# Products of q, k and v as three 16-bit products of high and low parts

## The reference

```python
x = x + attention(layernorm(x))
    proj = x @ w_qkv                    # 512 x 1536, split into q, k, v
    q, k = rope(q), rope(k)             # 16 heads of 32
    q, k = layernorm(q), layernorm(k)   # per head, with scale and bias
    a = tril((q @ k.T) ** 4)
    out = (a / a.sum(-1)) @ v
    out = out @ w_out
x = x + experts(layernorm(x))           # 4 of 16 experts a row, and a shared one
```

## Time and profile before

| | us |
|---|---|
| median of 3 runs (lowest, highest) | 1075.78 (1074.30, 1088.98) |
| the profiled execution | 1074.49 |
| its span, from first to last instruction | 1072.7 |
| busy PE, DVE, ACT, POOL in the span | 949.1, 718.1, 571.4, 523.3 |
| product matmuls of L515, busy | 184.2 |

### The profile page before, as it was taken

How to read it: one execution, slowest core, us unless ns; L and a number is a source line. 1 busy time by engine, 2 the same in 40 slices (tenths; PEclk the granted TensorE clock), 3 DMA queues, 4 the chain that set the end, 5 groups by cost and what they waited for, 6 DMA issues and landing times.

```text
span 1072.7 us, 21356 instructions
## 1 busy us (share of the span) xinstructions
PE 949.1 (88%) x5818; PEld 459.0 (43%) x5819; DVE 718.1 (67%) x1635; ACT 571.4 (53%) x1044; POOL 523.3 (49%) x738
## 2 busy tenths in 40 slices
PE   7989999899899989787787899999999999979892
PEld 5443334334443435242354445454544444434440
DVE  3888976887879688749658675565666555545552
ACT  2368984888838984976254234343444443324340
POOL 0007663665526563757201014666676665646642
PEclk9999999999999999857969999999999999999996
DMA  8113334443324433943457988898999897869884
GB/s 305 82 40 118 119 119 143 152 139 136 122 99 158 158 118 128 385 153 124 157 189 247 315 314 214 215 227 209 224 223 228 198 221 200 208 155 219 194 197 68
DMA packets 76795, 193.57 MB, mean 180 GB/s; under 512 B 10048, under 2 KB 11200, under 8 KB 75456
## 3 DMA queue, kind: packets, MB, share of 16 engines
q1 hardware_dynamic: 58816, 149.57, 41.9%
q0 software_dynamic: 17920, 43.26, 20.1%
HBM read 131.71 MB, written 61.10 MB: 180 GB/s over the span
## 4 chain that ended last, share of the span: by engine, by line
PE 37%; DVE 14%; issue 12%; ACT 10%; DMA 10%; POOL 6%; POOLq 4%; DVEq 4%; ACTq 0%; SPq 0%
DMA out<-yy,sidx 9%; PE bank L786 9%; PE bank L515 8%; PE bank L589 5%; PE bank L578 4%; PE bank L807 4%; ACT arena L960 3%; POOL wr L1157 2%; POOLq L1200 2%; PE bank L530 2%; PE bank L777 1%; ACT s_p L952 1%; POOLq L1156 1%; DVE st L1271 1%; POOL s_p L1132 1%
## 5 line engine op out<-in xcount | busy, mean ns | idle before, releaser
L786 PE MATMUL bank<-arena,xgT 128*128 (+1 forms) x1152 | 284.4, 384 | 4.3 <-ACT xgT L1094 3.4
L1132 POOL TENSOR_TENSOR s_p<-s_p,c_causal 128x128 f32<-128x128 f32 x256 | 148.7, 604 | 218.0 <-DVE s_p L1512 186.9
L1087 ACT ACTIVATE hT<-bank 128x512 f16<-128x512 f16 x96 | 57.3, 597 | 289.7 <-PE bank L796 268.6
L515 PE MATMUL bank<-arena 128*128 128x512 f32 x384 | 184.2, 628 | 11.6 <-ACT arena L921 4.6
L1140 POOL TENSOR_TENSOR arena<-arena 128x768 f16<-128x768 f32 x68 | 116.6, 1714 | 95.4 <-ACT arena L864 95.0
L786 PEld LDWEIGHTS bank<-arena,xgT 128*128 128x128 f16 x1152 | 108.2, 98 | 128.0 <-issue 38.1
L1181 POOL DMA_INDIRECT out<-yy,sidx x80 | 128.5, 1606 | 37.6 <-issue 29.2
L807 PE MATMUL bank<-wd,hT 128*128 128x512 f16 x576 | 142.1, 383 | 0.7 <-ACT hT L1087 0.7
L1799 DVE TENSOR_SCALAR yy<-bank,hsc 128x512 f32<-128x512 f32 x80 | 60.0, 751 | 122.9 <-DMA out<-yy,sidx 122.9
L960 ACT ACTIVATE arena<-bank 128x512 f32<-128x512 f32 (+3 forms) x256 | 101.2, 439 | 59.3 <-PE bank L563 59.2
L515 PEld LDWEIGHTS bank<-arena 128*128 128x128 f32 x384 | 73.2, 199 | 102.9 <-issue 88.9
(11 more groups left out here) (187 smaller groups left out, 1398.1 us busy)
## 6 DMA issues: line engine op xcount, KB each, us to landing
wd<-w_scratch SPq DMA_DIRECT2D x82, 512.0 KB
arena<-w_experts SPq DMA_DIRECT2D x34, 768.0 KB, 5.9
w_scratch<-arena SPq DMA_DIRECT2D x34, 768.0 KB, 4.5
arena<-w_scratch SPq DMA_DIRECT2D x17, 1024.0 KB, 7.4
xin<-x SPq DMA_DIRECT2D x4, 1024.0 KB, 5.5
arena<-x SPq DMA_DIRECT2D x4, 1024.0 KB, 5.5
x_scratch<-arena SPq DMA_DIRECT2D x4, 1024.0 KB, 5.1
xg<-xn_scratch SPq DMA_DIRECT2D x16, 256.0 KB, 4.3
```

The lines of the kernel that those rows point to most:

```text
L515: mm = pe.matmul(bk[:], xnT[:, c, m * P:m * P + P], wqkv[:, c, w * E:w * E + E], start=(c == 0), stop=(c == EC - 1))
L786: mm = pe.matmul(bank[2 + k][:], xgT[:, k, xh * EC + c, :], w, start=(c == 0 and xh + wh == 0), stop=(c == EC - 1 and xh == 1))
L1132: pool.tensor_tensor(d, d, C["causal"][:], ALU.mult).then_inc(p4_masked, 1)
```

## The change

Each product becomes three products of 16-bit numbers: high rows with high weights, high rows with low weights, low rows with high weights. The area of `xnT` and `wqkv` holds the high and the low part where it held the fp32 number. The weights and the rows are scaled by powers of two (256 for the weights, `WS`; 1024 for the rows, `XS`), which is taken back where v is copied and by the constants added under the roots.

```diff
             def qkv(b, m, w, bk, done):
-                pe.wait_ge(xT_sb, upto(b, m))
+                pe.wait_ge(xT_lo, upto(b, m))
                 for c in range(EC):
-                    mm = pe.matmul(bk[:], xnT[:, c, m * P:m * P + P], wqkv[:, c, w * E:w * E + E],
-                                   start=(c == 0), stop=(c == EC - 1))
+                    for xh, wh in ((0, 0), (0, 1), (1, 0)):
+                        mm = pe.matmul(bk[:], xnT[:, xh, c, m * P:m * P + P], wqkv[:, wh, c, w * E:w * E + E],
+                                       start=(c == 0 and xh + wh == 0), stop=(c == EC - 1 and xh == 1))
                 mm.then_inc(done, 1)
...
+            def first_lo(b, m, bk):
+                dve.wait_ge(xT_sb, upto(b, m))
+                dve.tensor_tensor(xnT[:, 1, :, m * P:m * P + P], quad(bk), xnT[:, 0, :, m * P:m * P + P],
+                                  ALU.subtract).then_inc(xT_lo, 1)
...
             def ahead(b, i):
+                if i == 11 and lb < B:
+                    first_lo(lb, 0, bkA)
+                elif i == 13 and lb < B:
+                    first_lo(lb, 1, bkB)
+                elif i == 14 and lb < B:
+                    first_lo(lb, 2, bkB)
...
             def behind(b, i):
                     if m:
                         finish(b, m - 1)
                         split_qk(nb, m - 1)
+                    elif b:
+                        first_lo(nb, 3, bkA)
                     head_variance(nb, m)
```

The weights are loaded in three transfers, for q, k and v, into areas that are free at that time (`w32`), ahead of the constants on SP's queue as before. ACT makes the high parts, DVE the low parts of q's and k's weights; for v's, ACT scales in place and POOL subtracts:

```diff
+            def weight_hi(w):
+                act.wait_ge(wqkv_in[w], 16)
+                act.activation(wqkv[:, 0, :, w * E:w * E + E], w32[w], ACT.Copy, scale=WS).then_inc(wqkv_hi, 1)
+
             deviation(1)
+            weight_hi(0)
             first_norm(1, (0, 1))
             copy_first(0, 0, bank[4])
+            weight_hi(1)
             first_norm(1, (2,))
             copy_first(0, 1, bank[5])
             first_norm(1, (3,))
+            weight_hi(2)
+            act.wait_ge(wqkv_hi, 3)
+            act.activation(w32[2], w32[2], ACT.Copy, scale=WS).then_inc(wv_scaled, 1)
             copy_first(0, 2, bank[4])
...
+            pool.wait_ge(wv_scaled, 1)
+            pool.tensor_tensor(wqkv[:, 1, :, 2 * E:3 * E], w32[2], wqkv[:, 0, :, 2 * E:3 * E], ALU.subtract).then_inc(wv_lo, 1)
...
+            def weight_lo(w):
+                dve.wait_ge(wqkv_hi, w + 1)
+                dve.scalar_tensor_tensor(out=wqkv[:, 1, :, w * E:w * E + E], in0=w32[w], scalar=WS,
+                                         in1=wqkv[:, 0, :, w * E:w * E + E], op0=ALU.mult, op1=ALU.subtract
+                                         ).then_inc(wqkv_lo, 1)
```

More of the change, by code:

```diff
@@ L167, in build @@
         split16 = lambda a: a.bitcast(F16).rearrange("p g (h n) -> p h g n", h=2)
-        wqkv = low(0, EC * 3 * E).rearrange("p (a b) -> p a b", a=EC)
+        wqkv = low(0, EC * 3 * E).bitcast(F16).rearrange("p (h a b) -> p h a b", h=2, a=EC)
         attT = [low(3, NG * N).rearrange("p (a b) -> p a b", a=NG), over([NG, N])]
@@ L172, in build @@
         wout = over([EC, E])
-        xnT = over([EC, N])
+        xnT = split16(over([EC, N]))
         s_sq = over([HG, N])
@@ L261, in build @@
         oct16 = lambda bk: bk[:].bitcast(F16).rearrange("p (c n) -> p c n", c=8)
-        consts_in, wqkv_in, wout_in, experts_in = map(sem, ("consts_in", "wqkv_in", "wout_in", "experts_in"))
+        consts_in, wout_in, experts_in = map(sem, ("consts_in", "wout_in", "experts_in"))
+        wqkv_in = [sem("wq_in"), sem("wk_in"), sem("wv_in")]
+        wqkv_hi, wqkv_lo, wv_scaled, wv_lo = map(sem, ("wqkv_hi", "wqkv_lo", "wv_scaled", "wv_lo"))
+        xT_lo = sem("xT_lo")
         stage_in = [sem("stage_in0"), sem("stage_in1")]
@@ L334, in _ @@
             sp.dma_start(C["ident"][:], cst["ident"]).then_inc(ident_in, 16)
-            sp.dma_start(wqkv, w_qkv).then_inc(wqkv_in, 16)
+            for w in range(3):
+                sp.dma_start(w32[w], w_qkv[:, :, w * E:w * E + E]).then_inc(wqkv_in[w], 16)
             for k, v in cst.items():
@@ L727, in _ @@
                         pe.wait_ge(read, upto(0, m - 1))
+                    else:
+                        pe.wait_ge(wqkv_lo, w + 1)
                     qkv(0, m, w, bank[w], done)
@@ L740, in _ @@
                     pe.wait_ge(v_sb, upto(0, m - 1))
+                else:
+                    pe.wait_ge(wv_lo, 1)
                 qkv(0, m, 2, bank[2], v_ps)
@@ L909, in deviation @@
                 act.wait_ge(var1, n)
-                act.activation(first[:, 0, :], mv[:, :, 1], ACT.Sqrt, bias=eps[:, 0:1]).then_inc(std1, 1)
+                act.activation(first[:, 0, :], mv[:, :, 1], ACT.Sqrt, bias=eps_x[:, 0:1], scale=1.0 / (XS * XS)
+                               ).then_inc(std1, 1)
             def first_norm(n, ms):
@@ L920, in copy_first @@
                 act.wait_ge(xT_ps, upto(b, m))
-                act.activation(xnT[:, :, m * P:m * P + P], quad(bk), ACT.Copy).then_inc(xT_sb, 1)
+                act.activation(xnT[:, 0, :, m * P:m * P + P], quad(bk), ACT.Copy).then_inc(xT_sb, 1)
             def copy_v(b, m, bk):
@@ L926, in copy_v @@
                     act.wait_ge(xn2_out, 16 * (b - 1))
-                act.activation(vtok[b % 2][:, m, :], bk[:], ACT.Copy).then_inc(v_sb, 1)
+                act.activation(vtok[b % 2][:, m, :], bk[:], ACT.Copy, scale=1.0 / (XS * WS)).then_inc(v_sb, 1)
             def head_squares(b, m):
@@ L934, in head_deviation @@
                 act.wait_ge(hvar, upto(b, m))
-                act.activation(hs[:, 1, :], hs[:, 0, :], ACT.Sqrt, bias=eps[:, 0:1], scale=1.0 / D).then_inc(hstd, 1)
+                act.activation(hs[:, 1, :], hs[:, 0, :], ACT.Sqrt, bias=eps_qk[:, 0:1], scale=1.0 / D).then_inc(hstd, 1)
             def row_deviation(b):
@@ L1115, in _ @@
             pool.memset(eps[:], EPS)
+            pool.memset(eps_x[:], EPS / (XS * XS))
+            pool.memset(eps_qk[:], EPS * (XS * WS) ** 2)
             pool.memset(ones[:], 1.0)
@@ L1631, in sequence @@
                 add_residual(b)
+            def weight_lo(w):
[3 more added lines that the diff above has]
+                                         ).then_inc(wqkv_lo, 1)
             first_norm_stats(1)
             first_norm(1)
+            weight_lo(0)
+            first_lo(0, 0, bank[4])
+            weight_lo(1)
+            first_lo(0, 1, bank[5])
             dve.wait_ge(consts_in, 16 * NCST)
@@ L1645, in _ @@
                 rope_k(0, m, bank[1])
-                if m == 2:
+                if m == 0:
+                    first_lo(0, 2, bank[4])
+                    first_lo(0, 3, bank[5])
+                elif m == 2:
                     first_norm(2)
+                elif m == 3:
+                    first_lo(1, 0, bkA)
                 centre(0, m)
@@ L1659, in _ @@
             split_qk(0, 3)
+            for m in range(1, MB):
+                first_lo(1, m, bank[m - 1])
             centre(1, 0)
```

24 lines of the change are left out of this document (12 added, 12 removed).

## The result

The changed kernel took 1092.88 us (median of 4 runs, 1088.78 to 1094.2), the kernel before beside it 1077.02 (4 runs). The ratio is 1.0146, with a 95% interval of 1.0107 to 1.0185: it became 1.5% slower. The forecast was 1075.6 with a range of 1061 to 1087, so the time lies above the range; within 2% is the one thing that held. The profiled execution took 1092.32 us, its span 1090.5.

The account below looks back on a forecast made before the run. In the attention steps PE, DVE and ACT were taken as nearly full, in the opening DVE's serial chain as the bound. 1074.49 + 6.7 (opening) - 5.6 (steps) = 1075.6 us, range 1061 to 1087.

Parts of the forecast that it names:

- The product: One row block with one third of the weights: 3.43 us before, 2.58 after, saving 0.85 at the high clock.
- Faster matmuls in a stream: Rival: 16-bit matmuls pace faster, a product saves 54%, 36 of 66.8 us go; 1045 us, chance 0.01.
- The opening: Making q, k and v of batch 0, 14 to 76 us: 6.7 us longer, bounds 2.1 and 8.4.
- The three low parts at the end: End of the opening: three subtractions of 0.69 us before the scores, 1.3 us later, between 0.7 and 2.1.
- The steps: Attention of batches 0 to 2: half the saving, 8.4 us, less 2.8 for low parts, so 5.6 us shorter.
- the upper end: Attention of batches 0 to 2: chained products only shrink, gaining 25% of 66.8 us, 16.7 us.
- The place that I had worked out: Steps 8 to 10 of batch 0: four products save 3.4 us, of which 0.9, a quarter, are left.
- The low parts: Eight DVE subtractions in the three attention stretches, 5.5 us; half exposed, 2.8 us, bounds 0 and 5.5.
- The clock: Rival: emptier PE falls to the low clock in the steps, 20 us longer; 1095.6 us, chance 0.09.
- Nothing arrives: Rival: in the steps only a quarter of the saving arrives, all low parts exposed; 1082.5 us, chance 0.18.

Follow-up runs that it names:

- no_lo_pool_after: Changed kernel without the rows' low parts (third matmul takes high rows again), POOL's subtraction in steps 4, 8 and 12 waiting for DVE's split; ratio 0.9970 to the kernel before.
- pool_after: Changed kernel with all its work, POOL's subtraction in steps 4, 8 and 12 waiting until DVE's split is done; ratio 1.0053 to the kernel before.

## Why the prediction was wrong, point by point

**The product** was right: twelve matmuls take 2.75 us from the first one's start to the last one's end, where eight fp32 records took 3.70, both at the high clock. Faster matmuls in a stream, the rival at 1045, did not show.

**The opening** was right in its order and near in its size, 4.9 for 6.7. ACT's pass took 1.90 (1.95 forecast), DVE's weight subtraction 2.29 (2.7), POOL's 4.06 (4.5): the prices for 2048 elements taken from 512 and 768 were too high, and POOL ended at 25.94, not 27.0. The squares are 4.0 us late, not 5.2. The three low parts at the end took 1.88 and PE's wait there went from 2.59 to 3.65, so 1.06 for the 1.3 taken. Without low parts the opening takes 79.5, so about 3.3 us are the weights' and 1.6 the rows'.

**The steps** were wrong, and that is the step that failed: "Between a quarter and all I take half, 8.4 us." The products did leave the chain, 24 us of it, more than the 16.7 that I took for the upper end. But in the profiled stretches nothing of it arrived (352.3 against 352.8 without low parts). In batch 0 each product with nothing else behind it gave its whole saving: steps 2, 8 and 10 went from 5.50, 6.70 and 6.40 to 4.56, 5.77 and 5.60. The place that I had worked out came near: steps 8 to 11 of batch 0 are together 1.2 us shorter (0.9 forecast). Step 6 gave back what they gained, since the work of DVE and ACT there has its own length and DVE's split met POOL's subtraction. I had asked how full the engines are, and not which instruction of DVE stands beside which of POOL's; the trace of before shows the margin that was to be lost in batch 0, 0.35 us. But with the meeting gone only 1.2 to 3.4 us of the saving arrive. That DVE and ACT hold the rest is read from one place of one trace; no run shows it for the other steps.

**The low parts** are the second term that failed, "I take half as exposed, 2.8", with 5.5 as the bound. They cost 11.1 us of the profiled stretches, and 8.1 where the products keep their old length. By the times of the two kernels with POOL behind, they cost 1.0053 - 0.9970, 8.9 us give or take 3.5, with the opening's 1.6. The bound was wrong because it took their work alone as the cost: a low part also holds the bank that PE transposes into (4.3 us of PE's waits), and the product waits for it (6.6 us, where it waited 4.3 for ACT's copy). And it shifts DVE's work against POOL's: two of the changed kernel's four stretched splits lie in batch 0, and without low parts batch 0 has none.

**The clock**, the rival at 1095.6, is part of it. It should decide from a mean of 0.86 and the mean fell to 0.91 (111.8, 133.3 and 118.3 us at 0.92, 0.88 and 0.93), which by the rival's own sum is 33 us lost in place of 13. The products' own busy time in the stretches fell by 18.6 us (133.6 to 115.0) in place of 28.9. The products at 167.5 us of the changed kernel and at 226.9 us of no_lo_pool_after show it on the chain, some 2.5 us each. How much of the 11.5 it makes by itself isn't settled: the kernels that keep it up also change when the products end.

**Nothing arrives**, at 1082.5, had the right sign and held both mechanisms, a quarter of the saving and all of the low parts, at too small a price. That pool_after took 1082.08 is luck: its opening is 5.3 us longer than before, not 6.7, and its profiled stretches 5.6, not 1.3. Of the whole forecast the difference within 2% held; the sign of the steps did not, and the range was too low at its top by 6 us.

No version was faster than the kernel before with the whole sum computed; the nearest, pool_after, is 0.5% slower, with an opening 5.3 us longer and profiled stretches 5.6 us longer.

## What to carry over

Before a saving on one engine is counted, look at what the other engines do at the same place: if one of them is busy for nearly the whole step (6.75 of 6.90 us here), the saving turns into idle time, and a matrix engine that idles may then run its next work at half rate. Look also at the margins between instructions of DVE and POOL that have both inputs in SBUF; a shift by a microsecond brought two of them together, and keeping them apart gave back 10.0 us (give or take 4.9). Such a meeting was dear where a result that others wait for stood behind it, and cheap where it didn't. An added instruction costs its own time, and the time for which it holds a buffer that another engine wants to fill.

## What the runs showed of the hardware

POOL and DVE, with both inputs of DVE in SBUF, shut each other out for whole instructions, and the one that began first goes on (POOL's, begun 1.00 us into two splits, left them at 1.28 us). While POOL subtracted from 21.88 to 25.94 us, DVE's low parts (one input in PSUM, one in SBUF) took 0.64 us each, as ever; the centring behind them (both inputs in SBUF) took 3.03 where it takes 1.23, and ended 1.08 after POOL, about its own length. The split did the same (2.73 for two in place of 1.28), and a cast of 0.23 took 2.41. POOL's subtraction that began during the first of two splits took 1.93 in place of 1.65.
The Trainium skill ("SBUF — State Buffer", section "Who interferes with whom") states that a DVE instruction with two SBUF inputs contends with a GpSimd instruction that reads SBUF, that casts can too, and that the later one fully blocks; the trace agrees in all three, with 3.03, 2.73 and 2.41 us. Had I held that page against the change, the question of what meets what would have been asked.
